# Attention inside a fused decoder block: where two pieces of the next x are staged, and which of VectorE's two jobs comes first

## The chip, the cores and the metric

One NeuronCore of a Trainium2 chip runs the whole program in one launch. The metric is device time in microseconds, of which lower is better. A core has TensorE (PE), VectorE (DVE), ScalarE (ACT), GpSimd (POOL) and SyncE (SP, which here only issues DMAs). Each engine works through its own list in order; they meet through semaphores.

## The reference

A pre-norm block in fp32: x (4 x 1024 x 512) goes through causal attention (16 heads of 64), a memory layer and a top-2 mixture of experts. The change touches only the attention:

```python
x = x + attn(layernorm(x), W_qkv, W_out)
# attn: qkv = x @ W_qkv; q, k = rotary(q), rotary(k)
# scores = q @ k.T / 8; masked above the diagonal; weights = softmax(scores)
# out = weights @ v
```

## The kernel before

fp32 products are made of fp32r halves: every operand is split into a high part (ScalarE copies it to fp32r) and a low part (the raw value minus the high part, on GpSimd or VectorE), and three matmuls stand for one.

**Units.** The attention runs over 512 units `u`. Eight units (one for each 128-row query tile, in the order 7, 0, 6, 1, 5, 2, 4, 3) are a head; 32 units are a group of 4 heads; 128 units are a batch row. I write `w` for a unit's place in a group's 32. In unit u TensorE makes the scores of u (L878 to L880), turns the probabilities of unit u-2 by transposes (`turn`, L891), does a slice of the next q/k or v projection (`fill`, L828 to L830) and, for half of the units, multiplies a pair of tiles with v (`values`, L908). VectorE takes the row maximum of u (`rowmax`, L1100), ScalarE the exponential of u (`exps`, L1015), and the turned probabilities of u-2 are split by ScalarE (`part_high`, L1026) and VectorE (`part_low`, L1109).

**Pairs.** A head has four pairs. The even ones (j = 0, 2) are multiplied at the end of units 5 and 1 (mod 8), ahead of the scores of the next unit; the odd ones right behind the scores of units 7 and 3. In the unit that follows an even product ScalarE copies half of the result (`out_low`, L1032) and VectorE adds the other (`out_add`, L1124), which frees the PSUM bank `O`; every `values` waits for the `out_add` before it.

**The next x.** In the last group of a batch row (three times in the run) the four 512 KB pieces of the next row's normalized, transposed x are loaded, split and put into `xT`. Raw data, x and weights alike, pass through `raw`, which has two slots: GpSimd issues the load of piece k+2 only when piece k has been split (`load`, called in `low`). ScalarE makes an x piece's high part (`high`, L989), VectorE its low part (`x_low`, L1061). The pieces sit at w = 8, 9, 10 and 11. The next q projection starts at w = 12 and waits for all four pieces; the first v steps are at w = 13.

**Rotation.** `rope_mult` (VectorE), `rope_add` (GpSimd, L734 and L735), `rope_high` (ScalarE) and `rope_low` (GpSimd) use the buffers `tmp` and `part`. In the last group of a row the last projection ends at w = 6, its last `rope_add` is in GpSimd's w = 7 and its last `rope_low` in w = 9.

Of the kernel before, what the change touches and what calls it, by code (L numbers as in the profile page):

```python
# [6 lines left out]
F32 = mybir.dt.float32  # L7
# [4 lines left out]
ALU = mybir.AluOpType  # L12
# [3 lines left out]
P = 128  # L16
# [3 lines left out]
ET = D // P  # L20
# [377 lines left out]
def attention_phase(nc, io, dram, scan, early):  # L398

    with Room(nc, "a_") as rm:  # L400
# [38 lines left out]
        s_sc = rm.sem("sc")  # L439
        s_mem = rm.sem("mem")  # L440
        s_load = [rm.sem(f"load{i}") for i in range(2)]
        s_high = rm.sem("high")
        s_wlow = rm.sem("wlow")
        s_xlow = rm.sem("xlow")
# [53 lines left out]
        def values_turn(u):  # L498

            for j, d in enumerate(TURN):  # L500
                if u >= d and (u - d) % QT == 0 and (u - d) // QT < NG * GH:
                    return (u - d) // QT * (QT // 2) + j
            return None
# [63 lines left out]
        def zbank(z):  # L567
            return Z[zi[z] % 2]

        def splits(u):  # L570

            n, w = u // GU, u % GU
            out = []
            if n + 1 < NG:
                if w == 2:
                    out.append(("wv", n + 1))
                if w == 7:
                    out.append(("wq", 2 * n + 2))
                if n % G == G - 1 and 8 <= w < 8 + ET:
                    out.append(("x", n // G + 1, w - 8))  # L580
                if w == 23:
                    out.append(("wq", 2 * n + 3))
            return out

        pieces = [("wq", 1)]
        for u in range(U):
            pieces += splits(u)
        pidx = {p: k for k, p in enumerate(pieces)}
        wcount, xcount = {}, {}
        for p in pieces:  # L590
            if p[0] == "x":
# [13 lines left out]
        def x_rows(z):  # L605

            return (z[1] // (G * GH // 2)) if z[0] == "q" else z[1] // G
# [81 lines left out]
        def _(gp):  # L689
# [4 lines left out]
            gp.memset(identb[:, :], 0.0).then_inc(s_pool, 1)  # L694
            gp.memset(maskb[:, :], 0.0).then_inc(s_pool, 1)

            def load(k):
                p = pieces[k]
                if k >= 2:
                    q = pieces[k - 2]  # L700
                    if q[0] == "x":
                        gp.wait_ge(s_xlow, xcount[q])
                    else:
                        gp.wait_ge(s_wlow, wcount[q])
                if p[0] == "x":
                    for i in range(2):
                        gp.wait_ge(s_xst[i], 16 * QT * p[1])
                    src = dram["xnT"][p[1], p[2] * P:(p[2] + 1) * P, :]
                elif p[0] == "wq":
                    src = io["wqk"][pair_of(p[1])]  # L710
                else:
                    src = io["wv"][p[1] % G]
                gp.dma_start(raw[:, k % 2, :], src).then_inc(s_load[k % 2], 16)

            def low(p):
                k = pidx[p]
                if p[0] != "x":
                    hi, lo = target(p)
                    gp.wait_ge(s_high, k + 1)
                    gp.tensor_tensor(lo, raw[:, k % 2, :], hi.bitcast(F32), ALU.subtract).then_inc(s_wlow, 1)  # L720
                if k + 2 < len(pieces):
                    load(k + 2)

            load(0)
            load(1)
# [11 lines left out]
            def rope_low(i, c):  # L737
                cols = slice(c * 512, (c + 1) * 512)
                for r in range(2):
                    gp.wait_ge(s_rhi, 4 * i + 2 * c + r + 1)  # L740
                    gp.tensor_tensor(rot[:, 2 + r, cols], tmp[:, c, r, :], rot[:, r, cols].bitcast(F32),  # L741
                                     ALU.subtract).then_inc(s_rot, 1)
# [57 lines left out]
            for u in range(U):  # L800
                for i, j in ends(q_steps(u - 1), 4):
                    if j % 2:
                        rope_add(i, j // 2)
                for i, c in rope_turn(u):
                    rope_low(i, c)
                for p in splits(u):
                    low(p)
                if tile_in(u, 5) is not None:
                    norm_tile(tile_in(u, 5))
                if u == U - 16:  # L810
                    load_next()
                if u == 9:
                    context_start()
                if u % (2 * QT) in (11, 14):
                    context_row(2 * (u // (2 * QT)) + u % (2 * QT) // 14)
# [7 lines left out]
        def _(pe):  # L823
# [3 lines left out]
            def split_mm(out, lhs, rhs, start, stop):  # L827
                pe.matmul(out, lhs(0), rhs(0), start=start, stop=False)  # L828
                pe.matmul(out, lhs(0), rhs(1), start=False, stop=False)  # L829
                return pe.matmul(out, lhs(1), rhs(0), start=False, stop=stop)  # L830

            def z_ready(z):
                if zi[z] >= 2:
                    pe.wait_ge(s_zfree, zi[z] - 1)
                if z[0] in ("q", "v"):
                    x, w = ("x", x_rows(z), ET - 1), ("wq" if z[0] == "q" else "wv", z[1])
                    if x in xcount:
                        pe.wait_ge(s_xlow, xcount[x])
                    if w in wcount:
                        pe.wait_ge(s_wlow, wcount[w])  # L840

            def project(i, k):


                j, e = k // 4, k % 4
                c, a = j // 2, j % 2
                if e == 0:
                    z_ready(("q", i, j))
                mm = split_mm(zbank(("q", i, j))[:, :], lambda k: wq[:, k, e, a * P:(a + 1) * P],
                              lambda k: xT[:, k, e, c * 512:(c + 1) * 512], e == 0, e == ET - 1)  # L850
                if e == ET - 1:
                    mm.then_inc(s_zfull, 1)

            def project_v(n, k):

                j, tt, e = k // 8, k // 4 % 2, k % 4
                t = 2 * j + tt
                if k % 8 == 0:
                    z_ready(("v", n, j))
                mm = split_mm(zbank(("v", n, j))[:, tt * 256:(tt + 1) * 256],  # L860
                              lambda k: xT[:, k, e, t * P:(t + 1) * P], lambda k: wv[:, k, e, :],
                              e == 0, e == ET - 1)
                if k % 8 == 7:
                    mm.then_inc(s_zfull, 1)
# [108 lines left out]
        def _(act):  # L973
# [5 lines left out]
            def high(p):  # L979
                k = pidx[p]  # L980
                hi, lo = target(p)
                act.wait_ge(s_load[k % 2], 16 * (k // 2 + 1))
                if p[0] == "x" and p[1]:
                    act.wait_ge(s_zfull, zi[("q", p[1] * G * GH // 2 - 1, 3)] + 1)
                if p[0] == "wq" and p[1]:
                    act.wait_ge(s_zfull, zi[("q", p[1] - 1, 3)] + 1)
                if p[0] == "wv" and p[1]:
                    act.wait_ge(s_zfull, zi[("v", p[1] - 1, 3)] + 1)
                act.activation(hi, raw[:, k % 2, :], ACT.Copy).then_inc(s_high, 1)  # L989

            def rope_high(i, c):
                act.wait_ge(s_radd, 4 * i + 2 * c + 2)
# [61 lines left out]
        def _(dve):  # L1054
            dve.wait_ge(s_tab, 2)

            def x_low(p):
                k = pidx[p]
                hi, lo = target(p)
                dve.wait_ge(s_high, k + 1)  # L1060
                dve.tensor_tensor(lo, raw[:, k % 2, :], hi.bitcast(F32), ALU.subtract).then_inc(s_xlow, 1)  # L1061

            def rope_mult(i, j):
                c, a = j // 2, j % 2
# [55 lines left out]
            def out_add(k):  # L1120
                dve.wait_ge(s_otmp, k + 1)
                if k >= 4:
                    dve.wait_ge(s_ost[k % 4], 16 * (k // 4))
                dve.tensor_tensor(ot[:, k % 4, :], O[0:HD, 0:2 * P], otmp[:, :], ALU.add).then_inc(s_ofree, 1)  # L1124
# [3 lines left out]
            for j in range(4):  # L1128
                v_low(0, j)
            for u in range(U + 6):  # L1130
                if u < U:
                    rowmax(u)
                if values_turn(u - 1) is not None:
                    out_add(values_turn(u - 1))
                if tile_in(u, 4) is not None:
                    tile_stats(tile_in(u, 4))
                for a in range(2):
                    if tile_in(u, 10 + 4 * a) is not None:
                        tile_out(tile_in(u, 10 + 4 * a), a)
                for i, j in ends(q_steps(u - 1), 4):  # L1140
                    rope_mult(i, j)
                if sums_turn(u) is not None:
                    sums(sums_turn(u))
                for n, j in ends(v_steps(u - 2), 8):
                    v_low(n, j)
                if 2 <= u < U + 2:
                    part_low(u - 2)
                if u < U:
                    for p in splits(u):
                        if p[0] == "x":  # L1150
                            x_low(p)
# [1019 lines left out]
```

## Time and profile before

| what | value |
| --- | --- |
| median of 3 runs | 2990.51 us (2986.48 to 2994.03) |
| profiled execution | 2990.0 us |
| its span | 2988.3 us |
| TensorE busy | 2731.2 us (91%) |
| VectorE, ScalarE, GpSimd busy | 1978.7, 1663.8, 1491.8 us |
| attention, about | 65 to 1700 us of the span |

The span is the time from the first to the last instruction; 1.7 us lie around it. TensorE is close to full, so what can be had is in its idle gaps. In a timeline row the first two numbers are start and duration; a bracket is the engine's idle time just before, with what ended it.

### The profile page before, as it was taken

Reading aid. Unit: us, or ns where it says so; the run is one execution under the profiler, and the core shown is the slowest. Engines: PE = TensorE matmul, PEld = TensorE weight load, DVE = VectorE, ACT = ScalarE, POOL = GpSimd, SP = SyncE. Lnnn points to the kernel's source line nnn. Section 1 sums busy time; section 2 is a strip of 40 time slices with the busy share of each in tenths; the row PEclk is TensorE's granted clock in tenths of the full one; section 3 lists DMA queues with packets and bytes.
Section 4 is the critical chain, followed back from the end, with each engine's and each line's share of the span. In section 5 each row is a group of like instructions: output and inputs, shape, how many; then the busy total and the mean of one; then the engine's idle time right before and its main releaser. Section 6 shows DMA issues by size and latency. Waiting matters only on the chain. (4 is left out here: it accounts for less than half of the span.)

```text
span 2988.3 us, 49627 instructions
## 1 busy us (share of the span) xinstructions
PE 2731.2 (91%) x15887; PEld 2292.6 (77%) x15887; DVE 1978.7 (66%) x3727; ACT 1663.8 (56%) x3193; POOL 1491.8 (50%) x1681
## 2 busy tenths in 40 slices
PE   5899989999989999899999689999959999999997
PEld 3788868888868888788888568778747888888886
DVE  5476766666756766566766669888845666666665
ACT  2456565656556656556666533333316676666665
POOL 1567555666646576546464434444423444444444
PEclk8999999999989999999999899999979999999999
DMA  3544443353534443433342555555433434444432
GB/s 123 106 115 106 105 117 91 91 128 87 123 87 108 101 120 92 122 90 89 91 102 62 155 154 153 142 142 143 125 129 67 99 81 99 99 99 99 99 56 49
DMA packets 193144, 316.79 MB, mean 106 GB/s; under 512 B 60896, under 2 KB 107008, under 8 KB 189888
## 3 DMA queue, kind: packets, MB, share of 16 engines
q1 hardware_dynamic: 147920, 214.94, 29.0%
q0 software_dynamic: 43952, 97.46, 13.3%
q8 instruction: 94, 1.54, 0.2%
q10 hardware_dynamic: 1088, 2.11, 0.2%
q14 instruction: 90, 0.74, 0.1%
HBM read 244.42 MB, written 75.17 MB: 107 GB/s over the span
## 5 line engine op out<-in xcount | busy, mean ns | idle before, releaser
L1026 ACT ACTIVATE a_pt<-a_PT 128x512 fp32r<-128x512 f32 (+3 forms) x768 | 350.4, 490 | 538.2 <-PE a_PT L891 537.4
L1100 DVE TENSOR_REDUCE a_nmax<-a_S 128x1 f32<-128x1024 f32 (+7 forms) x512 | 384.4, 751 | 273.3 <-PE a_S L880 272.0
L1109 DVE TENSOR_TENSOR a_pt<-a_PT,a_pt 128x512 fp32r<-128x512 f32 (+3 forms) x768 | 401.3, 549 | 191.4 <-ACT a_pt L1026 189.7
L908 PE MATMUL a_O<-a_pt,a_v 128*128 128x256 f32 (+1 forms) x2560 | 358.0, 287 | 49.2 <-DVE a_ot L1124 25.0
L1015 ACT ACTIVATE a_pb<-a_S,a_nmax 128x1024 f32<-128x1024 f32 (+7 forms) x512 | 380.3, 743 | 18.4 <-DVE a_nmax L1100 18.3
L908 PEld LDWEIGHTS a_O<-a_pt,a_v 128*128 128x128 f32 x2560 | 327.9, 194 | 64.4 <-DVE a_ot L1124 30.7
L891 PE MATMUL a_PT<-a_ident,a_pb 128*128 128x128 f32 x2304 | 342.6, 276 | 33.6 <-DVE a_pt L1109 32.3
L2068 DVE TENSOR_TENSOR e_w<-early_stage,e_w 128x1024 fp32r<-128x1024 f32 x238 | 280.8, 1219 | 121.5 <-ACT e_w L2018 121.4
L891 PEld LDWEIGHTS a_PT<-a_ident,a_pb 128*128 128x128 f32 x2304 | 270.9, 142 | 77.0 <-issue 28.5
L878 PE MATMUL a_S<-a_kh,a_qs 128*128 128x512 f32 (+3 forms) x768 | 285.8, 372 | 4.2 <-DMA a_kl<-a_rot 4.2
L828 PE MATMUL a_Z<-early_xT,early_wq 128*128 128x512 f32 x512 | 240.2, 469 | 44.1 <-issue 15.7
L879 PE MATMUL a_S<-a_kl,a_qs 128*128 128x512 f32 (+3 forms) x768 | 259.0, 349 | 0.0
L741 POOL TENSOR_TENSOR a_rot<-early_stage,a_rot 128x512 fp32r<-128x512 f32 x128 | 162.9, 1291 | 178.3 <-ACT a_rot L997 178.0
L1904 POOL DMA_INDIRECT out<-e_y,e_dest x78 | 159.1, 2040 | 182.9 <-ACT e_y L2027 167.4
L2018 ACT ACTIVATE e_w<-early_stage 128x2048 fp32r<-128x2048 f32 x119 | 227.6, 1912 | 40.4 <-DMA early_stage<-in_we,e_ix 39.8
L734 POOL TENSOR_TENSOR early_stage<-early_stage,a_part 128x512 f32<-128x512 f32 x64 | 82.3, 1286 | 313.6 <-DVE a_part L1075 313.6
L1900 POOL DMA_INDIRECT early_stage<-in_we,e_ix x122 | 153.6, 1259 | 155.8 <-issue 137.2
L830 PE MATMUL a_Z<-early_xT,early_wq 128*128 128x512 f32 x512 | 204.3, 399 | 0.0
L829 PE MATMUL a_Z<-early_xT,early_wq 128*128 128x512 f32 x512 | 203.8, 398 | 0.0
L878 PEld LDWEIGHTS a_S<-a_kh,a_qs 128*128 128x128 f32 x768 | 147.4, 192 | 24.2 <-DMA a_kl<-a_rot 6.5
L828 PE MATMUL a_Z<-early_wv,early_xT 128*128 128x256 f32 x512 | 163.1, 319 | 2.0 <-DVE a_v L1092 2.0
L879 PEld LDWEIGHTS a_S<-a_kl,a_qs 128*128 128x128 f32 x768 | 147.7, 192 | 17.4
(296 smaller groups left out, 6995.2 us busy)
## 6 DMA issues: line engine op xcount, KB each, us to landing
a_qs<-a_rot SPq DMA_DIRECT2D x256, 128.0 KB, 2.3
a_kh<-a_rot SPq DMA_DIRECT2D x256, 128.0 KB, 2.3
a_kl<-a_rot SPq DMA_DIRECT2D x256, 128.0 KB, 2.3
e_rows<-scr_hs SPq DMA_DIRECT2D x40, 516.0 KB
scr_attT<-a_ot SPq DMA_DIRECT2D x256, 64.0 KB, 2.1
m_att<-scr_attT SPq DMA_DIRECT2D x32, 512.0 KB
m_rb<-scr_rinv SPq DMA_DIRECT2D x64, 256.0 KB
early_stage<-in_wqk POOLq DMA_DIRECT2D x31, 512.0 KB, 4.2
```

The lines of the kernel that those rows point to most:

```text
L828: pe.matmul(out, lhs(0), rhs(0), start=start, stop=False)
L830: return pe.matmul(out, lhs(1), rhs(0), start=False, stop=stop)
L878: pe.matmul(out, q, kh[:, sl, c0:c1], start=True, stop=False)
L879: pe.matmul(out, q, kl[:, sl, c0:c1], start=False, stop=c1 != cols)
L891: mm = pe.transpose(PT[(k + s) % 2][:, (kt % 4) * P:(kt % 4 + 1) * P], pb[u % 2][:, kt * P:(kt + 1) * P], ident[:, :])
L908: mm = pe.matmul(O[:, c0:2 * P], v2[:, n % 2, kt, h, :, :].rearrange("p a d -> p (a d)"), pt[j % 2][:, part, kt, c0:2 * P], start=kt == 0 ...
L1015: act.activation(pb[u % 2][:, 0:cols], S[u % 2][:, 0:cols], ACT.Exp, bias=nmax[:, u % GU:u % GU + 1], scale=1.0, accum_out=rsum[:, b % 2, ...
L1026: act.activation(pt[u % 2][:, 0, 4 * s:4 * s + m, (qt % 2) * P:(qt % 2 + 1) * P], PT[(k + s) % 2][:, 0:m * P].rearrange("p (k q) -> p k q" ...
L1100: dve.tensor_reduce(nmax[:, u % GU:u % GU + 1], S[u % 2][:, 0:cols], AXX, ALU.max, negate=True).then_inc(s_nb, 1)
L1109: dve.tensor_tensor(pt[u % 2][:, 1, 4 * s:4 * s + m, q], PT[(k + s) % 2][:, 0:m * P].rearrange("p (k q) -> p k q", k=m), pt[u % 2][:, 0, 4 ...
L2018: act.activation(w[:, k, 0, :], raw[:, k, :], ACT.Copy).then_inc(s[f"whi{k}"], 1)
L2068: dve.tensor_tensor(w[:, k, 1, c], raw[:, k, c], w[:, k, 0, c].bitcast(F32), ALU.subtract).then_inc(s[f"wlo{k}"], 1)
```

## The change

Pieces 1 and 2 of the next x no longer pass through `raw`: they are loaded in w = 6 and 7 into `tmp[:, 0]` and `part`, which the rotation has finished with by then, with semaphores of their own. Pieces 0 and 3 stay in `raw`. The splits sit at w = 7, 9, 10 and 11 instead of 8 to 11. The projections wait for each piece where its first matmul needs it, not for the last piece at their start. On VectorE `out_add` of an even pair is placed before the unit's `rowmax`; odd pairs are as before.

```diff
+        XSPLIT = (7, 9, 10, 11)
-                if n % G == G - 1 and 8 <= w < 8 + ET:
-                    out.append(("x", n // G + 1, w - 8))
+                if n % G == G - 1 and w in XSPLIT:
+                    out.append(("x", n // G + 1, XSPLIT.index(w)))
+        by_raw = [p for p in pieces if p[0] != "x" or p[2] in (0, 3)]
+        ridx = {p: k for k, p in enumerate(by_raw)}
+        def source(p):
+            if p in ridx:
+                return raw[:, ridx[p] % 2, :]
+            return (tmp[:, 0, :, :] if p[2] == 1 else part[:, :, :]).rearrange("p a n -> p (a n)")
+            def load_x(b, e):
+                i = b * G * GH // 2 - 1
+                if e == 1:
+                    gp.wait_ge(s_rot, 4 * i + 2)
+                else:
+                    gp.wait_ge(s_radd, 4 * i + 4)
+                gp.dma_start(source(("x", b, e)), x_rows_of(("x", b, e))).then_inc(s_xload[e - 1], 16)
...
+                b, w = u // (GU * G) + 1, u % (GU * G) - GU * (G - 1)
+                if b < B and w in (6, 7):
+                    load_x(b, w - 5)
                 for p in splits(u):
                     low(p)
...
+            def x_ready(z, e):
+                x = ("x", x_rows(z), e)
+                if x in xcount and z[2] == 0:
+                    pe.wait_ge(s_xlow, xcount[x])
...
             for u in range(U + 6):
+                k = values_turn(u - 1)
+                if k is not None and k % 2 == 0:
+                    out_add(k)
                 if u < U:
                     rowmax(u)
-                if values_turn(u - 1) is not None:
-                    out_add(values_turn(u - 1))
+                if k is not None and k % 2:
+                    out_add(k)
```

## Rows read from the trace of the kernel before

**Rows 1.** Engines' busy time by stretch, then PEclk, DMA share, GB/s.

```profile
90.00:425.00 335.00, 309.70 (x2073) 267.15 (x2072) 222.12 (x411) 195.14 (x465) 201.12 (x252) 0.98 0.47 110
425.00:452.00 27.00, 16.65 (x83) 14.81 (x84) 13.22 (x20) 13.09 (x26) 14.81 (x19) 0.75 0.60 161
```

**Rows 2.** What PE waited for, 90 to 1700 us: total, times, longest us.

```profile
PE a_PT L891 <- DVE a_pt L1109: 32.3, 44, 8.8
PE a_O L908 <- DVE a_ot L1124: 25.0, 37, 4.6
PE a_Z L828 <- issue: 15.7, 3, 5.4
PE a_O L908 <- DVE a_xt L1087: 14.5, 23, 0.8
...
PE a_O L908 <- issue: 8.8, 24, 0.4
...
PE a_S L878 <- DMA a_kl<-a_rot: 4.2, 6, 1.6
```

**Rows 3.** Timeline of PE in units 43 and 47, an ordinary head.

```profile
235.81 0.23 PE L880 MATMUL a_S<-a_maskb,a_identb 128*128 128x128 bf16 x1
236.41 1.12 PE L908 MATMUL a_O<-a_pt,a_v 128*128 128x256 f32 x8 [0.37 <-issue]
...
249.11 0.23 PE L880 MATMUL a_S<-a_maskb,a_identb 128*128 128x128 bf16 x1
249.15 0.65 PE L908 MATMUL a_O<-a_pt,a_v 128*128 128x256 f32 x4
```

**Rows 4.** Timeline of DVE in unit 42 of the same head.

```profile
234.89 1.09 DVE L1100 TENSOR_REDUCE a_nmax<-a_S 128x1 f32<-128x896 f32 x1 [1.27 <-PE a_S L880]
235.90 0.41 DVE L1124 TENSOR_TENSOR a_ot<-a_O,a_otmp 64x256 f32<-64x256 f32 x1
```

**Rows 5.** Timeline of ACT in unit 42.

```profile
234.80 0.38 ACT L1032 ACTIVATE a_otmp<-a_O 64x256 f32<-64x256 f32 x1
...
236.37 1.01 ACT L1015 ACTIVATE a_pb<-a_S,a_nmax 128x896 f32<-128x896 f32 x1
```

**Rows 6.** Timeline of DVE at the first change of x, w = 8 to 9.

```profile
423.54 1.20 DVE L1100 TENSOR_REDUCE a_nmax<-a_S 128x1 f32<-128x1024 f32 x1
424.67 0.87 DVE L1109 TENSOR_TENSOR a_pt<-a_PT,a_pt 128x512 fp32r<-128x512 f32 x2
426.96 2.18 DVE L1061 TENSOR_TENSOR early_xT<-early_stage,early_xT 128x1024 fp32r<-128x1024 f32 x1 [1.42 <-ACT early_xT L989]
...
433.18 1.23 DVE L1061 TENSOR_TENSOR early_xT<-early_stage,early_xT 128x1024 fp32r<-128x1024 f32 x1 [3.24 <-ACT early_xT L989]
```

**Rows 7.** Timeline of ACT there, w = 7 and w = 11.

```profile
422.51 1.05 ACT L989 ACTIVATE early_wq<-early_stage 128x1024 fp32r<-128x1024 f32 x1
...
442.12 1.06 ACT L989 ACTIVATE early_xT<-early_stage 128x1024 fp32r<-128x1024 f32 x1 [2.30 <-DMA early_stage<-scr_xnT]
```

**Rows 8.** Timeline of POOL there.

```profile
424.46 1.26 POOL L735 TENSOR_TENSOR early_stage<-early_stage,a_part 128x512 f32<-128x512 f32 x1
425.69 2.37 POOL L720 TENSOR_TENSOR early_wq<-early_stage,early_wq 128x1024 fp32r<-128x1024 f32 x1
428.35 0.58 POOL L713 DMA_DIRECT2D early_stage<-scr_xnT  x1 [0.30 <-POOL early_wq L720]
...
436.72 0.58 POOL L713 DMA_DIRECT2D early_stage<-scr_xnT  x1
```

**Rows 9.** Timeline of PE there, w = 9 to 12.

```profile
425.49 0.92 PE L891 MATMUL a_PT<-a_ident,a_pb 128*128 128x128 f32 x4 [1.25 <-DVE a_pt L1109]
426.06 2.80 PE L908 MATMUL a_O<-a_pt,a_v 128*128 128x256 f32 x12
...
435.79 1.87 PE L908 MATMUL a_O<-a_pt,a_v 128*128 128x256 f32 x8 [4.63 <-DVE a_ot L1124]
...
444.54 0.77 PE L828 MATMUL a_Z<-early_xT,early_wq 128*128 128x512 f32 x1 [5.23 <-issue]
```

More of the change, by code:

```diff
@@ L441, in attention_phase @@
         s_load = [rm.sem(f"load{i}") for i in range(2)]
+        s_xload = [rm.sem(f"xload{i}") for i in range(2)]
         s_high = rm.sem("high")
@@ L695, in _, with x_rows_of @@
             gp.memset(maskb[:, :], 0.0).then_inc(s_pool, 1)
+            def x_rows_of(p):
+                for i in range(2):
+                    gp.wait_ge(s_xst[i], 16 * QT * p[1])
+                return dram["xnT"][p[1], p[2] * P:(p[2] + 1) * P, :]
+            def load_x(b, e):
[5 more added lines that the diff above has]
+                gp.dma_start(source(("x", b, e)), x_rows_of(("x", b, e))).then_inc(s_xload[e - 1], 16)
             def load(k):
-                p = pieces[k]
+                p = by_raw[k]
                 if k >= 2:
-                    q = pieces[k - 2]
+                    q = by_raw[k - 2]
                     if q[0] == "x":
@@ L705, in load @@
                 if p[0] == "x":
-                    for i in range(2):
-                        gp.wait_ge(s_xst[i], 16 * QT * p[1])
-                    src = dram["xnT"][p[1], p[2] * P:(p[2] + 1) * P, :]
+                    src = x_rows_of(p)
                 elif p[0] == "wq":
@@ L715, in low @@
             def low(p):
-                k = pidx[p]
                 if p[0] != "x":
                     hi, lo = target(p)
[L719 to L722, printed above, removed]
+                    gp.wait_ge(s_high, pidx[p] + 1)
+                    gp.tensor_tensor(lo, source(p), hi.bitcast(F32), ALU.subtract).then_inc(s_wlow, 1)
+                if p in ridx and ridx[p] + 2 < len(by_raw):
+                    load(ridx[p] + 2)
             load(0)
@@ L835, in z_ready @@
                 if z[0] in ("q", "v"):
-                    x, w = ("x", x_rows(z), ET - 1), ("wq" if z[0] == "q" else "wv", z[1])
-                    if x in xcount:
-                        pe.wait_ge(s_xlow, xcount[x])
+                    w = ("wq" if z[0] == "q" else "wv", z[1])
                     if w in wcount:
                         pe.wait_ge(s_wlow, wcount[w])
+            def x_ready(z, e):
+                x = ("x", x_rows(z), e)
+                if x in xcount and z[2] == 0:
+                    pe.wait_ge(s_xlow, xcount[x])
             def project(i, k):
@@ L848, in project @@
                     z_ready(("q", i, j))
+                x_ready(("q", i, j), e)
                 mm = split_mm(zbank(("q", i, j))[:, :], lambda k: wq[:, k, e, a * P:(a + 1) * P],
@@ L859, in project_v @@
                     z_ready(("v", n, j))
+                if k // 4 == 0:
+                    x_ready(("v", n, j), e)
                 mm = split_mm(zbank(("v", n, j))[:, tt * 256:(tt + 1) * 256],
@@ L981, in high @@
                 hi, lo = target(p)
-                act.wait_ge(s_load[k % 2], 16 * (k // 2 + 1))
+                if p in ridx:
+                    act.wait_ge(s_load[ridx[p] % 2], 16 * (ridx[p] // 2 + 1))
+                else:
+                    act.wait_ge(s_xload[p[2] - 1], 16 * p[1])
                 if p[0] == "x" and p[1]:
@@ L988, in high @@
                     act.wait_ge(s_zfull, zi[("v", p[1] - 1, 3)] + 1)
-                act.activation(hi, raw[:, k % 2, :], ACT.Copy).then_inc(s_high, 1)
+                act.activation(hi, source(p), ACT.Copy).then_inc(s_high, 1)
             def rope_high(i, c):
@@ L1060, in x_low @@
                 dve.wait_ge(s_high, k + 1)
-                dve.tensor_tensor(lo, raw[:, k % 2, :], hi.bitcast(F32), ALU.subtract).then_inc(s_xlow, 1)
+                dve.tensor_tensor(lo, source(p), hi.bitcast(F32), ALU.subtract).then_inc(s_xlow, 1)
             def rope_mult(i, j):
```

## The prediction, made before the changed kernel was run

> **What bounds the kernel now.** I read the views from wide to narrow. The page's first part says that TensorE is the fullest engine, and busy time by stretch says that it is fuller still in ordinary attention (309.7 of 335 us) but not in the 27 us in which x changes (16.7 of 27, at a mean granted clock of 0.75) [rows 1]. So the bound is TensorE, and a change is worth the idle time that it takes from TensorE, plus what the lower of the two clock levels (1.2 instead of 2.4 GHz) costs behind long gaps. The view of waits then names the gaps [rows 2]. Two of them belong to this diff. The multiplications with v wait for VectorE's `out_add` (25.0 us in 37 places, three of them long) and in 24 more places for "issue" (8.8 us). And the first projection on the new x waits three times, 15.7 us together. The largest entry, transposes behind `part_low` (32.3 us), is touched only by side effects, and the wait on L1087 (14.5 us) not at all: it sits in units 5 (mod 8), behind the row maximum of an odd unit.
>
> Last I read the timelines of all engines side by side, once in an ordinary head and once where x changes.
>
> **Part 1, out_add of even pairs.** In unit 42 VectorE is idle for 1.27 us, then takes the row maximum at 234.89 and adds at 235.90 [rows 4]. The copy that the addition needs was finished by ScalarE at 234.80 + 0.38 = 235.18 [rows 5]. TensorE ends the scores of unit 43 with the L880 at 235.81 and starts the v product only at 236.41, 0.10 behind the end of `out_add` [rows 3, 4]. Its row says "issue", but nothing else is late: I count these 24 places with the others. What is lost is not the gap of 0.37 alone, since the durations of matmuls are modelled and overlap: from L880 to L908 it is 0.60 us start to start here and 0.04 in unit 47, where nothing is waited for [rows 3]. So a gap of 0.37 costs 0.56, 0.19 more than it shows.
>
> In the new order the addition goes first: 235.2 to 235.6, so the product may start at about 235.7, and TensorE is not there before 235.85. The wait goes entirely, though with 0.15 us in hand in this kind of head (ScalarE has rotation copies ahead of L1032); in heads without them the copy is earlier and there is more. The 37 places less the three long ones have 25.0 minus 3 x 4.5, or 11.5 us; with 8.8 that is 20.3 us in 58 places, 0.35 each, and with 0.19 added 0.54. 58 x 0.54 = 31 us.
>
> What the move puts behind: the row maximum starts at 235.6 rather than 234.89 and ends near 236.65; the exponential started at 236.37 because ScalarE was still on `part_high`, so it becomes 0.3 us later [rows 4, 5]. Who waits for that? The scores of unit 44 need it, 2.2 us after it ends, and the transposes of unit 42 come later still. The row maximum of unit 43 and its `part_low` are pushed by 0.3 too, and are back behind ScalarE within two units, since VectorE idles there. Unit 6 (mod 8) has the other even pair: its next product is in unit 7 and has no wait now, so nothing is won, and the row maximum is 0.1 later, at no price. What is not returned by these queues can be returned by DMA: at six head starts the scores already wait for the stacked k and q, 4.2 us in all [rows 2]. There the stack follows GpSimd's rotation, not TensorE, and the 0.5 us is given back: five such places, +2.5 us.
>
> **Part 2, the change of x, three times.** Before, TensorE stands for 1.25, 4.63 and 5.23 us [rows 9]. The chain behind the long two is the ring through `raw`: load at 428.35 once the wq piece is split, split, load at 436.72, split at 442.12 after a DMA wait of 2.30, `x_low`, projection at 444.54 [rows 7 to 9]. And the `x_low`s, waiting on VectorE ahead of row maxima, hold `out_add` back; that is the gap of 4.63.
>
> The new loads of pieces 1 and 2 go out at about 419.7 and 425.9 (two issues of 0.58, in w = 6 and in w = 7 behind L735; the split of wq and all after it on GpSimd start some 0.6 later), that of piece 3 at about 429.5 instead of 436.72. The first load of before took 3.7 us to landing (ScalarE took piece 1 up at 432.1), the last 5.4 us beside the stack's DMAs. So the pieces land at about 423.5, 430 and 434: none is waited for any more. What is left is the order in the queues. From w = 7 on, with durations from the rows:
>
> Piece 0 now comes in w = 7. ScalarE makes its high part behind that of wq, 423.5 to 424.6 [rows 7]. VectorE's `x_low` then meets GpSimd's L735, which runs to 425.7 [rows 8]. In before one `x_low` met GpSimd's L720 and took 2.18 us, to 1.1 us behind its end; with GpSimd idle or later it took 1.23 [rows 6, 8]. I take the first: `x_low` ends at 426.9, the row maximum of w = 8 (1.20) at 428.0, the first `part_low` at 428.6. So the transposes that started at 425.49 start at 428.6: this edit costs 3.1 us here, and the gap of 1.25 becomes about 4.4. The Trainium skill (SBUF — State Buffer, section "SBUF: two separate sides") says that a VectorE instruction with two SBUF inputs and a GpSimd instruction that reads SBUF exclude each other for a whole instruction. The 2.18 agrees. Without such a lock the transposes would start at about 427.5 and the sum would be 3 us lower; with it, as the row has it, the sum stands.
>
> From there: 12 products (2.8 at the low clock) to 432.0; scores, eight transposes, scores (2.4 as before) to 434.3. `out_low` comes behind the rotation copies at 432.5, `out_add`, now ahead of the row maximum, ends at 433.3, so the 4.63 is gone, and the product starts at 434.3 instead of 435.79. It takes 1.87, a transpose and the scores of w = 12 take 1.7: the projection starts at about 437.7 instead of 444.54, 6.8 earlier, for only piece 0 is needed. The transposes of w = 10 then wait on `part_low`, behind `x_low` of piece 2, to about 438.7, and the last piece is ready near 441, where the v steps ask for it at 441 too. If TensorE stays at the low clock for all of this the gain shrinks to about 6; if it has the full clock again from about 433 it grows to 9. I take 7.5, between the two, since the gaps before it are shorter but not gone: 3 x 7.5 = 22.5 us. The extra semaphore waits in the projections find pieces that are there, but for this last one.
>
> **Sum.** Profiled 2990.0 (0.5 under the median of the runs): 2990.0 - 31 - 22.5 + 2.5 = 2939. The phases behind the attention start when it ends, so they move with it.
>
> **The rivals.**
>
> B: the change of x brings little. Piece 0 in w = 7 stalls TensorE for 4.4 us, the clock drops there, and the chain of high part, low part, row maximum and exponential on VectorE and ScalarE takes the place of the loads. For it: VectorE and ScalarE both carry four more instructions of over 1 us in five units. Against it: 5.23 us of the stall are plainly a load. At 3 us per place: 2990 - 31 - 9 + 2.5 = 2952.
>
> C: the 31 us come back. A wait of 0.3 us removed on TensorE shows again at the next meeting with VectorE, such as the transposes behind `part_low` [rows 2], or the addition with 0.15 in hand is late after all. Against it: these waits follow TensorE's own scores at a fixed distance. With nothing of the 31 left: 2990 - 22.5 = 2967.
>
> D: the change of x leaves almost no gap, because `x_low` gets in before L735 and the full clock is kept: 12 us per place, 2990 - 31 - 36 + 2.5 = 2926.
>
> E, the other side: the addition, waiting for ScalarE at the head of VectorE's queue, holds up the row maximum, with it the exponential, and the scores two units later. Where the exponential is what TensorE waits for, 0.65 us are added in each of 64 units: +42, less 22.5, is 3010. It decides once the delay is over the 0.38 us that the exponential now waits anyway plus the 2.2 us before the scores; 0.65 is far below. Nothing at all (every gain returned) is 2990.
>
> **Chances.** Forecast 0.60, B 0.14, C 0.12, D 0.08, E 0.04, nothing 0.02. The forecast's own range is 2930 to 2948. With B and D whole and the near side of C the range is 2924 to 2960. 0.3% (9 us) is about what a measurement tells here: faster 0.94, same 0.03, slower 0.03.
>
> **What would show it.** Right: the wait of L908 on L1124 and "issue" all but gone from TensorE's waits; row maxima in units 2 (mod 8) starting right after L1124; near the first change of x a gap of about 4 us ahead of L891 in w = 9, none ahead of the following L908, the first L828 about 7 us nearer to it. Wrong: another wait of L891 or L878 that has grown by what L908 lost (C); L989 still waiting for DMA (the loads are late after all); a gap ahead of L891 over 6 us (B).

## The result, and the profile after

The changed kernel takes 2941.41 us (median of 4, 2937.66 to 2944.3), the kernel before 2988.49 us (median of 4): a ratio of 0.984, with a 95% interval of 0.9819 to 0.9862. Forecast were 2939 us and a range of 2924 to 2960. The profiled execution took 2944.3 us, its span 2942.5.

Of the changed kernel, TensorE's waits from 90 to 1660 us (total, times, longest):

```profile
PE a_PT L925 <- DVE a_pt L1146: 50.5, 54, 11.7
PE a_O L942 <- DVE a_xt L1124: 15.3, 24, 0.8
PE a_Z L856 <- DVE early_stage L1112: 12.9, 24, 2.1
PE a_Z L856 <- DVE a_v L1129: 5.3, 3, 1.8
PE a_S L912 <- DMA a_kl<-a_rot: 3.7, 3, 3.0
PE a_S L912 <- ACT a_pb L1052: 1.5, 5, 0.4
PE a_O L942 <- DVE a_ot L1161: 0.9, 1, 0.9
```

Against [rows 2], the product's waits on `out_add` and "issue" went from 33.8 us to 0.9, and the 15.7 us of the first projection on the new x are gone. L1124 is the same wait as L1087 there and has not moved. What grew is the transposes' wait on `part_low`, from 32.3 to 50.5 us. Of these 18.2 us, 14 lie where x changes, as the timelines show, and 3.0 in a single wait of the second head (8.8 us before, 11.7 after), for which I have no cause.

An ordinary head first, unit 43 on TensorE, then unit 42 on VectorE and ScalarE:

```profile
235.91 0.23 PE L914 MATMUL a_S<-a_maskb,a_identb 128*128 128x128 bf16 x1
235.95 1.13 PE L942 MATMUL a_O<-a_pt,a_v 128*128 128x256 f32 x8
```

```profile
235.31 0.42 DVE L1161 TENSOR_TENSOR a_ot<-a_O,a_otmp 64x256 f32<-64x256 f32 x1 [1.59 <-ACT a_otmp L1069]
235.65 1.07 DVE L1137 TENSOR_REDUCE a_nmax<-a_S 128x1 f32<-128x896 f32 x1
```

```profile
236.76 1.01 ACT L1052 ACTIVATE a_pb<-a_S,a_nmax 128x896 f32<-128x896 f32 x1 [0.17 <-DVE a_nmax L1137]
```

The product follows the last matmul of the scores by 0.04 us, where it was 0.60 [rows 3]. The addition stands ahead of the row maximum, ScalarE now waits 0.17 us for the maximum, and nothing of that reaches TensorE here: in the traces 46 of the 63 heads that can be compared are 0.47 to 0.57 us shorter, against 0.54 forecast. The last heads of the first three batch rows had no such wait and are as long as before.

Then the first change of x, w = 7 to 13, on VectorE and TensorE:

```profile
419.61 2.28 DVE L1098 TENSOR_TENSOR early_xT<-early_stage,early_xT 128x1024 fp32r<-128x1024 f32 x1 [0.93 <-ACT early_xT L1026]
421.81 1.21 DVE L1137 TENSOR_REDUCE a_nmax<-a_S 128x1 f32<-128x1024 f32 x1
422.95 0.87 DVE L1146 TENSOR_TENSOR a_pt<-a_PT,a_pt 128x512 fp32r<-128x512 f32 x2
```

```profile
423.77 1.09 PE L925 MATMUL a_PT<-a_ident,a_pb 128*128 128x128 f32 x4 [4.46 <-DVE a_pt L1146]
424.51 2.80 PE L942 MATMUL a_O<-a_pt,a_v 128*128 128x256 f32 x12
...
430.04 1.13 PE L942 MATMUL a_O<-a_pt,a_v 128*128 128x256 f32 x8
...
432.55 0.48 PE L856 MATMUL a_Z<-early_xT,early_wq 128*128 128x512 f32 x1
...
434.77 0.55 PE L925 MATMUL a_PT<-a_ident,a_pb 128*128 128x128 f32 x3 [0.84 <-DVE a_pt L1146]
...
438.61 0.41 PE L925 MATMUL a_PT<-a_ident,a_pb 128*128 128x128 f32 x2 [0.68 <-DVE a_pt L1146]
```

The gaps of 4.63 and 5.23 us [rows 9] are gone. The gap of 1.25 has become 4.46, behind `x_low` of piece 0 (2.28 us long), the row maximum and `part_low`, in that order. GpSimd and ScalarE show that the loads are no longer waited for:

```profile
418.31 1.27 POOL L759 TENSOR_TENSOR early_stage<-early_stage,a_part 128x512 f32<-128x512 f32 x1 [2.71 <-DVE a_part L1112]
419.55 1.25 POOL L760 TENSOR_TENSOR early_stage<-early_stage,a_part 128x512 f32<-128x512 f32 x1
421.10 0.58 POOL L723 DMA_DIRECT2D a_part<-scr_xnT  x1 [0.30 <-POOL early_stage L760]
421.70 2.40 POOL L745 TENSOR_TENSOR early_wq<-early_stage,early_wq 128x1024 fp32r<-128x1024 f32 x1
424.39 0.58 POOL L739 DMA_DIRECT2D early_stage<-scr_xnT  x1 [0.30 <-POOL early_wq L745]
```

```profile
434.69 1.04 ACT L1026 ACTIVATE early_xT<-early_stage 128x1024 fp32r<-128x1024 f32 x1
```

`x_low` began while L760 was under way and lasted until 1.1 us behind its end at 420.80. From the last matmul of the scores of w = 7 to that of w = 16 the three places took 43.3, 43.5 and 43.2 us before and take 37.0, 36.7 and 36.8 us now: 6.3 to 6.8 us each. Up to the scores of w = 13 it is 8.2 to 8.9, and 1.9 to 2.5 us of that are given back by w = 16: first at the gap of 0.68 above, which is new, then to the clock. TensorE waits 1.8 us in w = 15 for the low part of v, as it did before, but now runs at the lower of its two levels behind it, in all three places, where it had kept the full clock before. No run tells why. Busy time by stretch, with PEclk third from the end, of the changed kernel:

```profile
446.00:449.00 3.00, 1.22 (x7) 0.84 (x7) 1.60 (x3) 0.84 (x2) 2.41 (x8) 1.00 0.08 22
449.50:452.50 3.00, 3.00 (x9) 2.00 (x8) 0.85 (x2) 1.02 (x3) 1.86 (x2) 0.50 0.47 111
```

And of the kernel before, that wait (total, times, longest) and the stretch behind the first of the three:

```profile
PE a_Z L828 <- DVE a_v L1092: 5.3, 3, 1.8
```

```profile
462.00:465.00 3.00, 3.00 (x18) 2.33 (x17) 2.18 (x3) 1.28 (x4) 0.00 (x0) 1.00 0.81 190
```

### The profile page after: what moved, and what is told of

The parts are those of the page before. It is cut to its first block and busy times, and to the rows that moved or that the text cites. A ratio compares the mean times of both kernels' runs of the same rounds, so it can differ in the third digit from the quotient of the medians.

```text
span 2942.5 us, 49627 instructions
## 1 busy us (share of the span) xinstructions
PE 2716.7 (92%) x15887; PEld 2284.4 (78%) x15887; DVE 1982.5 (67%) x3727; ACT 1667.8 (57%) x3193; POOL 1491.9 (51%) x1681
## 5 line engine op out<-in xcount | busy, mean ns | idle before, releaser
L925 PE MATMUL a_PT<-a_ident,a_pb 128*128 128x128 f32 x2304 | 344.4, 277 | 51.7 <-DVE a_pt L1146 50.5
L942 PEld LDWEIGHTS a_O<-a_pt,a_v 128*128 128x128 f32 x2560 | 325.9, 193 | 23.6 <-DVE a_xt L1124 22.5
L1161 DVE TENSOR_TENSOR a_ot<-a_O,a_otmp 64x256 f32<-64x256 f32 x256 | 105.7, 413 | 184.0 <-ACT a_otmp L1069 183.9
```

Source lines behind the costliest of these rows:

```text
L925: mm = pe.transpose(PT[(k + s) % 2][:, (kt % 4) * P:(kt % 4 + 1) * P], pb[u % 2][:, kt * P:(kt + 1) * P], ident[:, :])
L942: mm = pe.matmul(O[:, c0:2 * P], v2[:, n % 2, kt, h, :, :].rearrange("p a d -> p (a d)"), pt[j % 2][:, part, kt, c0:2 * P], start=kt == 0 ...
```

## The experiments

Each expectation stands as it was written before its run. Edits are against the changed kernel unless said otherwise.

**e1: the order of `out_add` alone**, on the kernel before.

```diff
+                if k is not None and k % 2 == 0:
+                    out_add(k)
                 rowmax(u)
```

> Only the order of out_add and rowmax is changed; x is loaded and waited for as before. My theory: the wait of the v product on out_add costs 0.54 us start to start in 58 places and goes entirely; some 2.5 us come back where the stacked k and q arrive last. So 2988 - 31 + 2.5 = about 2960 (2955 to 2964), and the waits of L908 on out_add shrink to the three long ones at the change of x, about 13 us together. Rival (C of the prediction): the waits show again elsewhere and the x part earned all the gain; then 2980 or more here.

Measured: 2959.63 us, ratio 0.9911 (0.9895 to 0.9928). L908's wait on `out_add` is left at the changes of x:

```profile
PE a_Z L828 <- issue: 17.1, 3, 5.9
...
PE a_O L908 <- DVE a_ot L1124: 12.4, 4, 3.9
```

The time is as expected, to within a microsecond. Rival C is out. The 2.5 us that were to come back at the head starts are not seen: the scores' wait for the stacked k and q is 1.0 us in 2 places here, where it was 4.2 in 6.

**e2: the change of x alone**, `out_add` behind `rowmax` as before.

> Only the loads, splits and waits of the next x are changed; out_add stays behind rowmax everywhere. My theory: the trace of the changed kernel shows 6.3 to 6.8 us less per change of x between units w = 7 and w = 16; out_add behind the row maximum of w = 10 gives back about 0.5 of it. 2988 - 3 x 6 = about 2970 (2966 to 2974), with the 20 us of waits of L908 unchanged. Rival: the two parts need each other (the change of x pays only once out_add is early); then 2980 or more.

Measured: 2970.23 us, 0.9941 (0.9924 to 0.9958). 29.6 and 19.0 us apart make 48.6; both together made 47.1. The parts add; neither needs the other. As expected, the product's waits are unchanged: 11.3 us on `out_add` and 8.7 for "issue".

**e5: all four pieces waited for at once.**

```diff
-                x = ("x", x_rows(z), e)
+                x = ("x", x_rows(z), ET - 1)
```

> The changed kernel, but every projection on the new x waits for all four pieces, as in the kernel before. My theory: loads into idle buffers are what removes the stall of 5.2 us, but the last piece is split at 437.0 and the projection would start there instead of 432.55: 4.4 us later at each of three places, more where the clock falls: 2941 + 13 to 20, 2954 to 2961. Rival: the loads did it all and the finer waits are worth nothing: 2941.

Measured: 2952.14 us, 0.9874 (0.9857 to 0.989), 10.7 us over the changed kernel, a little under the range of 2954 to 2961. The wait that it brings back:

```profile
PE a_Z L856 <- DVE early_xT L1098: 13.2, 3, 4.4
```

**e6: the kernel before with the finer waits alone.**

> The kernel before with nothing but the finer waits: each matmul on the new x waits for its own piece. The ring through the two slots stays. My theory: piece 0 is ready at 429.1, piece 1 at 434.4, piece 2 at 438.9, so TensorE has some 5 us of work (two steps of the q projection, seven transposes, the scores, three steps of v) to put in front of the last piece at 444.4, and 3 x 5 = 15 us are won: about 2973 (2968 to 2979). Rival: the ring of loads is what costs, as the prediction put it; then 2985 to 2988 here.

Measured: 2981.42 us, 0.9976 (0.9966 to 0.9985): 7.8 us won and not 15. Its trace at the first change of x, v steps of w = 13:

```profile
446.04 0.38 PE L828 MATMUL a_Z<-early_wv,early_xT 128*128 128x256 f32 x1 [1.30 <-DVE early_xT L1067]
...
447.60 0.41 PE L897 MATMUL a_PT<-a_ident,a_pb 128*128 128x128 f32 x2 [0.94 <-DVE a_pt L1115]
```

TensorE did put its work ahead of the last piece, but then waited for it, and next for `part_low` behind the same `x_low`. Up to the scores of w = 13 the three places are 6.7 to 7.6 us shorter than before; 1.5, 5.3 and 2.8 of that are left at w = 16. Finer waits without new loads are worth 8 us, new loads without finer waits also some 8 (e5 is 7.5 us faster than e1, which has the same `out_add` and none of the rest), the two together 19.

**e3: piece 0 at w = 8**, `XSPLIT = (8, 9, 10, 11)`.

> The changed kernel with the split of piece 0 at w = 8 instead of 7. My theory: piece 0 at w = 7 is what makes the gap of 4.46 us ahead of the transposes of w = 9 (row maximum and part_low stand behind its x_low). At w = 8 that gap is back at about 1.25, but the x_low then stands ahead of the row maximum of w = 9 and part_low of w = 7, and pieces 0 and 1 come in adjacent units, so 1 to 2 us of the 3.2 come back: gain of 1 to 2 us per place, 2941 - 4.5 = about 2937 (2931 to 2942). Rival: the gap is only moved, nothing is won or 1 us is lost per place: 2941 to 2944.

Measured: 2937.82 us, 0.9831 (0.9815 to 0.9848). Its three places take 35.0, 36.4 and 35.1 us, 1.3 us less than the changed kernel's on average. The direction and size are those of the trace; the difference of 3.6 us in time alone would not be clear. What took the rest back is one instruction, on VectorE, with the wait on TensorE behind it:

```profile
420.82 3.16 DVE L1098 TENSOR_TENSOR early_xT<-early_stage,early_xT 128x1024 fp32r<-128x1024 f32 x1 [1.42 <-ACT early_xT L1026]
```

```profile
424.84 0.66 PE L925 MATMUL a_PT<-a_ident,a_pb 128*128 128x128 f32 x4 [2.12 <-DVE a_pt L1146]
```

The gap in w = 9 is 1.25 again, but `x_low` of piece 0 now starts 0.3 us into GpSimd's split of wq (L745, until 422.89) and takes 3.16 us, and the transposes wait 2.12 us behind it; the next product waits 1.77 for `out_add`.

**e8: `x_low` of piece 0 behind row maximum and `part_low` of w = 8.** ScalarE's part stays in w = 7.

```diff
+                    for p in splits(u - 1) if u else []:
+                        if p[0] == "x" and p[2] == 0:
+                            x_low(p)
                     for p in splits(u):
-                        if p[0] == "x":
+                        if p[0] == "x" and p[2]:
                             x_low(p)
```

> The changed kernel with one VectorE instruction moved: x_low of piece 0 stands behind row maximum and part_low of w = 8 instead of at the end of w = 7; ScalarE's part stays in w = 7. My theory: the gap of 4.46 us goes back to about 1.3 and x_low lies in VectorE's idle time behind it: 3 us per place, 2941 - 9 = 2932 (2928 to 2937), and the x_low of piece 0 no longer takes 2.28 us unless it meets GpSimd again. Rival: the gap of 4.46 is ScalarE's (two copies of 1.05 us ahead of part_high), not VectorE's: then nothing changes.

Measured: 2934.18 us, 0.981 (0.9794 to 0.9827). VectorE and TensorE:

```profile
415.41 1.20 DVE L1137 TENSOR_REDUCE a_nmax<-a_S 128x1 f32<-128x1024 f32 x1
416.90 0.89 DVE L1146 TENSOR_TENSOR a_pt<-a_PT,a_pt 128x512 fp32r<-128x512 f32 x2 [0.29 <-ACT a_pt L1063]
417.71 1.21 DVE L1098 TENSOR_TENSOR early_xT<-early_stage,early_xT 128x1024 fp32r<-128x1024 f32 x1
```

```profile
417.74 1.09 PE L925 MATMUL a_PT<-a_ident,a_pb 128*128 128x128 f32 x4 [1.63 <-DVE a_pt L1146]
```

The same instruction one place later in its queue takes the gap from 4.46 to 1.63 us; the three places take 33.8, 32.1 and 33.6 us. The gap stays 0.4 us above the 1.25 of before: `part_low` now waits 0.29 us for ScalarE, which has two copies ahead of its part. VectorE's order accounts for the rest. Starting behind the end of L760, `x_low` also took 1.21 us and not 2.28, so of the 2.8 us up to 1.1 are this stretch.

**e4: all low parts on GpSimd.**

> The changed kernel with the low parts of all four pieces made by GpSimd instead of VectorE. GpSimd is idle for 6.8 us behind w = 9 and takes 2.4 us for such a piece where VectorE takes 1.23. My theory: what is left at the change of x is VectorE's queue (x_low ahead of row maxima), so this takes the gap of 4.46 back to about 1.3, and the waits of 0.36, 0.84 and 0.68 with it: 3 to 5 us per place, 2941 - 12 = about 2929 (2925 to 2934). Rival: GpSimd's queue is the next limit (its rotation and the stack's DMAs come 2.4 us later, piece 3 is ready late) and nothing or little is won: 2938 to 2945.

Measured: 2938.46 us, 0.9832 (0.9815 to 0.9848); the rival's case. The three places take 37.1, 37.0 and 37.0 us, no less than the changed kernel's. The gap in w = 9 is 1.63 here too, but TensorE then waits for GpSimd, 12.6 us in 8 places:

```profile
PE a_Z L856 <- POOL early_xT L744: 12.6, 8, 2.5
```

GpSimd's queue at the first change (rotation, then pieces 1 to 3, 2.35 us each):

```profile
423.38 2.54 POOL L766 TENSOR_TENSOR a_rot<-early_stage,a_rot 128x512 fp32r<-128x512 f32 x2
425.88 2.35 POOL L744 TENSOR_TENSOR early_xT<-early_stage,early_xT 128x1024 fp32r<-128x1024 f32 x1
428.18 2.38 POOL L744 TENSOR_TENSOR early_xT<-a_part,early_xT 128x1024 fp32r<-128x1024 f32 x1
430.52 2.35 POOL L744 TENSOR_TENSOR early_xT<-early_stage,early_xT 128x1024 fp32r<-128x1024 f32 x1
```

The idle 6.8 us that I had counted on lie behind the rotation, while pieces 1 and 2 are wanted soon after it.

**e7: `out_add` first for odd pairs too.**

> The changed kernel with out_add ahead of rowmax for odd pairs too. For an odd pair the v product is issued behind the scores of the same unit, so the row maximum, whose scores are ready, has to wait for the product, ScalarE's copy and the addition: from the trace 1.5 to 2.5 us in 128 units. This tests rival E of the prediction, a row maximum held up by an addition: where the exponential then reaches TensorE late. My theory: the hold is now of the size of the 2.2 us in hand, so part of it shows: 0.5 to 1 us in each of 128 units, 2941 + 64 to 128, about 3030 (2970 to 3080). Rival: the order on VectorE does not matter at all: 2941.

Measured: 2950.62 us, 0.9872 (0.9856 to 0.9889): 9.2 us over the changed kernel, not 64 to 128, and below the expected 2970. I had misread the hold: the row maximum of an odd unit sits mostly behind other VectorE work anyway, and the addition held it for 0.3 us in unit 43 and 0.9 in unit 47, not 1.5 to 2.5. Ordinary heads are as long as in the changed kernel; 2.0 to 2.6 us are lost at each change of x, and 0.4 to 1.0 in two more heads of each of these rows. So this was no test of rival E. The next two are.

**e9 and e10: a dose for rival E.** The row maximum of units 2 and 6 (mod 8) is first taken once, or three times, into a spare buffer.

```diff
+                for _ in range(1 if u % QT in (2, 6) else 0):
+                    dve.tensor_reduce(pad[:, _ * 128 + u // 4:_ * 128 + u // 4 + 1],
+                                      S[u % 2][:, 0:cols], AXX, ALU.max, negate=True)
```

> The changed kernel, where in each unit with an even addition VectorE takes the row maximum once more into a spare buffer before the real one (the output is the same). This holds the real one up by 1.0 us in units 2 and 0.7 us in units 6 (mod 8), on top of what the addition does: a dose for rival E, which says that a row maximum held up reaches TensorE. My theory: from the end of the exponential of unit 2 to the scores that need it there are 1.4 us in the changed kernel, so a dose of 1.0 is absorbed there: 2941 to 2952. If E's mechanism were already at work, all of it would show: 64 x 1.7 = 109 us, 3050.

> As e9, but with three more row maxima: 3.0 us in units 2 and 2.2 us in units 6. My theory: now over the point from which it decides. In units 2 about 1.6 of the 3.0 us show, in units 6 (some 3 us in hand) little: 64 x 1.6 = 100 us, about 3040 (3000 to 3080). If there is more room than I read, under 2980; if all of it shows, 3270.

Measured: 2970.54 us (0.9942, 0.9927 to 0.9957) and 3158.53 us (1.0571, 1.0555 to 1.0587), that is 30.5 and 218.5 us over the changed kernel on the same chip. Both lie outside what was expected (2941 to 2952, 3000 to 3080). A dose of 109 us in all shows by 30, one of 333 by 218. That is less room than I read, it ends elsewhere, and it is not the same in every head. In e9's trace the second and fourth heads of a group (the last head of a row excepted) are 1.0 us longer than in the changed kernel's, all of it from unit 2's dose of 1.0, and nearly all others are as long as there; the 0.7 us in units 6 shows nowhere. So in nearly half of the heads TensorE has nothing in hand at unit 2, in the others more than 1.0 us (1.5 by e10's trace). e10's 218 us are not the dose alone: behind its longer gaps the granted clock falls (0.50 from 250 to 252 us, 0.952 over the run, against 0.967 in e9). In e9, VectorE in units 42 and 43, and TensorE in 43:

```profile
235.77 1.07 DVE L1139 TENSOR_REDUCE a_pad<-a_S 128x1 f32<-128x896 f32 x1
236.77 1.07 DVE L1141 TENSOR_REDUCE a_nmax<-a_S 128x1 f32<-128x896 f32 x1
237.76 0.67 DVE L1130 TENSOR_TENSOR a_v<-a_Z,a_v 128x512 fp32r<-128x512 f32 x1
238.36 1.27 DVE L1150 TENSOR_TENSOR a_pt<-a_PT,a_pt 128x512 fp32r<-128x512 f32 x2
```

```profile
239.18 0.30 PE L926 MATMUL a_PT<-a_ident,a_pb 128*128 128x128 f32 x1 [0.86 <-DVE a_pt L1150]
```

The same transpose in the changed kernel, with no gap:

```profile
238.06 0.30 PE L925 MATMUL a_PT<-a_ident,a_pb 128*128 128x128 f32 x1
```

It is not the exponential that comes late, as rival E and I both had it, but `part_low`, which stands behind the row maximum in VectorE's own queue, and on which the transpose of the next unit waits. Here VectorE has v's low part (L1130) between the two; in the head before, which loses nothing, it has not.

**e11: a faster version**, e8's order plus the low part of piece 2 alone on GpSimd (as in e4, with a semaphore of its own), beside **e12**, the changed kernel again.

> The changed kernel with x_low of piece 0 behind row maximum and part_low of w = 8 (as in e8) and with the low part of piece 2 alone made by GpSimd, which is idle from w = 10 on, under a semaphore of its own. In the trace of e8 two waits are left behind VectorE's queue at w = 12 and 13, 0.84 and 0.69 us. My theory: taking x_low of piece 2 out of VectorE's queue removes both, 1.5 us per place against e8, and 4.5 to 5 against the changed kernel with what e8 gave: 2941 - 3 x 4.5 = about 2928 (2924 to 2934). Rival: GpSimd's 2.4 us for the piece meet VectorE's x_low of piece 3 and the steps of v wait for them: not faster than e8, 2934 to 2937.

> The changed kernel itself, unchanged, beside e11 on the same chip, so that the difference of the two is not one between chips. All theories: 2938 to 2945.

Measured: 2927.74 us (2922.57 to 2931.91) and 2940.03 us (2938.39 to 2944.49), on one chip, whose kernel before took 2986.25: 0.9798 (0.9781 to 0.9814) and 0.984 (0.9827 to 0.9854). e11 is 12.3 us faster than the changed kernel and 58.5 than the one before. Its three places take 33.0, 31.4 and 32.6 us, 0.85 us less than e8's on average and not 1.5: the gap of 0.84 at w = 12 is gone, but its neighbour at w = 13 is 0.91, where e8 has 0.69.

## Why the prediction was right

**The additions, 31 us, less 2.5.** e1 measured 29.6 against 28.5. The term rested on counting the "issue" gaps with the others and on reading start to start instead of the gap shown; by the gaps alone it would have been 20. The 2.5 us that were to come back at the stack's DMAs are a term that no run shows: this wait fell from 4.2 us to 1.0 in e1, and the changed kernel has 3.7 us in 3 places, 3.0 of them at the last head alone.

**The change of x, 22.5 us.** e2 measured 19.0, and the trace has 6.3 to 6.8 us per place for my 7.5. Up to the w = 12 projection the schedule held. Shifted to the after trace (w = 7 began 4.9 us earlier there), it had the transposes at 423.7, the product at 429.4, the projection at 432.8; the trace has 423.77, 430.04 and 432.55. The gap of about 4.4 was 4.46, the stretched `x_low` 2.28. What I missed lies behind w = 13: 1.9 to 2.5 us per place are lost again by w = 16, to one more wait on `part_low` (0.68) and to the lower clock behind the old wait for the low part of v. Up to w = 13 the gain was above my 7.5. So the size of this term was off by 3 to 3.5 us, for what came after the stretch I had followed. The forecast gain was 51 us and the measured one 47; that the two times lie closer, 2939 and 2941, is partly luck, since I counted from 2990.0 and the median of the kernel before is 2988.49.

**The price of piece 0 in w = 7.** Costed at 3.1 us a place and said to be an order in VectorE's queue, with GpSimd's port in it. e8 shows it: 4.46 to 1.63 with that order alone. The stretched `x_low` is a part only of that, 1.1 of 2.8 us; e3, where `x_low` met a longer GpSimd instruction, won less.

**Rivals.** B (the change of x brings 3 us a place) and C (the 31 come back) are refuted by e2 and e1. D wanted a window with no gap; none of the versions came to 12 us at all three places, e11 being nearest with 10.3 to 12.1. E did not decide, but not by the margin I gave, and there was luck in it. I read 2.6 us in hand, to the scores behind the exponential. The doses show that the transposes behind `part_low` come first, and that in nearly every second head there is nothing in hand at unit 2 beyond the hold of about 0.65 us that the change brings. With 1 us more, e9, the 29.6 us of the additions are gone. The scores' wait on the exponential, E's own, is 1.5 us in 5 places in the changed kernel.

**What stays open.** The first two heads differ by up to 5 us between executions of similar kernels, which I didn't pursue. Why the clock falls behind the wait of w = 15, which is as long as before, is not shown. That GpSimd's work caused the 2.28 is inferred from the ends of the two instructions, in this run and the others; no run took that work away.

## What to carry to other kernels

When a wait on the bounding engine ends with an instruction of an engine that had been idle shortly before, look at that engine's queue first: one pair in the other order was worth 30 us here, and one instruction put behind two others 3.2 to 4.5 us in each place by the traces, 7 us in all by the time. Read the cost of a wait start to start against the same pair without it. And before moving work onto an idle engine, ask whether it is idle at the time the result is wanted: all four pieces on GpSimd won nothing at the three places, while the one that fitted won 0.85 us a place beside e8. Last, measure the room that a held instruction has with a dose, in every kind of head, and look at the heads one by one: the average, 1.2 us a head in e9, hid that nearly half of them had none.

## What the runs showed of the hardware

A wait ahead of a matmul costs TensorE more than the gap that the profile shows: 0.56 us for a gap of 0.37. A `tensor_tensor` on VectorE with both inputs in SBUF stretches when a GpSimd instruction reading SBUF is under way at its start. At the changes of x, over all runs, this happened to `x_low` 42 times: it took 1.40 to 3.16 us, and each time it ended 1.08 or 1.09 us after the GpSimd instruction. In the 111 other cases it took 1.21 to 1.23 us. The prediction took the 2.18 for its own case from the rows of before, and 2.28 was measured; e3's 3.16 shows that the stretch goes by what is left of the other instruction. The granted clock fell to 0.50 in the changed kernel both within the gap of 4.46 us (from about 422 to 428.5 us) and behind the wait of 1.8 us in w = 15, and not behind the same wait before.
